# VectorE's scan ahead of a reciprocal, moments a step earlier, and one normalised tile ahead of ScalarE's sigmoids

## What is computed

```python
x = x + 0.5 * ffn(layernorm(x), w_up, w_down)
x = x + rnn(layernorm(x), Wf, Wi, Wh)
x = x + 0.5 * ffn(layernorm(x), w_up, w_down)
```

## Time and profile before

| what | value |
|---|---|
| median of 3 runs | 279.79 us (277.55 to 280.13) |
| the profiled execution's own time | 279.18 us |
| its span in the trace | 277.5 us |
| TensorE busy | 242.3 us (87%) |
| VectorE busy | 234.5 us (85%) |
| ScalarE busy | 222.4 us (80%) |
| GpSimd busy | 218.0 us (79%) |

### The profile page before, as it was taken

How to read it: one execution, slowest core, us unless ns; L and a number is a source line. 1 busy time by engine, 2 the same in 40 slices (tenths; PEclk the granted TensorE clock), 3 DMA queues, 4 the chain that set the end, 5 groups by cost and what they waited for, 6 DMA issues and landing times.

```text
span 277.5 us, 9737 instructions
## 1 busy us (share of the span) xinstructions
PE 242.3 (87%) x3757; PEld 168.2 (61%) x3757; DVE 234.5 (85%) x741; ACT 222.4 (80%) x546; POOL 218.0 (79%) x394
## 2 busy tenths in 40 slices
PE   0578999999999998899999956669999999999983
PEld 0335777777777776555554524236777778767863
DVE  3668699999998999799999946678899999998784
ACT  1256999999999999588888863568999999999971
POOL 4888688988978775788888888897889999997131
PEclk9999999999999999999999999889999999999999
DMA  6990000000000000000000000000021121112213
GB/s 180 269 259 5 4 4 2 2 2 4 2 6 0 2 5 1 4 1 0 2 1 0 0 1 0 2 2 2 16 64 40 41 65 56 40 40 61 59 40 116
DMA packets 18046, 9.73 MB, mean 35 GB/s; under 512 B 592, under 2 KB 17872, under 8 KB 18000
## 3 DMA queue, kind: packets, MB, share of 16 engines
q1 hardware_dynamic: 16896, 8.39, 10.9%
q10 hardware_dynamic: 1104, 0.72, 0.9%
HBM read 4.92 MB, written 4.19 MB: 33 GB/s over the span
## 4 chain that ended last, share of the span: by engine, by line
PE 62%; DVE 11%; POOL 11%; issue 7%; ACT 7%; DMA 1%; POOLq 0%; DVEq 0%; ACTq 0%
PE Y L443 16%; PE U L403 9%; PE G L430 9%; PE U L404 8%; PE U L458 7%; PE T L384 6%; POOL root L192 4%; PE Y L458 3%; ACT h_hi L299 3%; DVE X L580 2%; POOL inject L231 2%; ACT U L293 2%; DVE h_lo L564 2%; PE G L422 2%; PE G L467 2%
## 5 line engine op out<-in xcount | busy, mean ns | idle before, releaser
L564 DVE SCALAR_TENSOR_TENSOR h_lo<-h_hi,U 128x1024 f16<-128x1024 f16 x64 | 77.1, 1216 | 11.3 <-ACT h_hi L299 10.9
L293 ACT ACTIVATE U<-U 128x1024 f32<-128x1024 f32 x64 | 65.6, 1025 | 17.7 <-PE U L404 16.8
L213 POOL TENSOR_SCALAR xn<-X,neg_mean,rstd 128x128 f32<-128x128 f32 x164 | 72.8, 457 | 4.7 <-DVE rstd L555 2.2
L299 ACT ACTIVATE h_hi<-U 128x1024 f16<-128x1024 f32 x64 | 65.8, 1027 | 1.1
L443 PE MATMUL Y<-down_w,h_hi 128*128 128x128 f16 x512 | 60.9, 220 | 0.0
L443 PE MATMUL Y<-down_w_half,h_lo 128*128 128x128 f16 x512 | 60.6, 219 | 0.0
L403 PE MATMUL U<-xt_hi,up_w 128*128 128x512 f16 x128 | 50.7, 396 | 6.3 <-DVE h_lo L564 4.1
L192 POOL TENSOR_TENSOR root<-mv,half 128x8 f32<-128x8 f32 (+1 forms) x26 | 50.4, 1940 | 2.2
L220 POOL TENSOR_TENSOR rms<-ssq,half 128x4 f32<-128x4 f32 x32 | 32.2, 1008 | 24.0 <-ACT square_junk L325 24.0
L404 PE MATMUL U<-xt_lo,up_w 128*128 128x512 f16 x128 | 50.5, 395 | 0.0
L443 PEld LDWEIGHTS Y<-down_w_half,h_lo 128*128 128x128 f16 x512 | 50.1, 98 | 0.0
(11 more groups left out here) (71 smaller groups left out, 383.6 us busy)
## 6 DMA issues: line engine op xcount, KB each, us to landing
X<-in_L_attn_x SPq DMA_DIRECT2D x16, 256.0 KB, 5.4
out_x<-X SPq DMA_DIRECT2D x16, 256.0 KB, 2.5
up_raw<-in_L_ffn_w_up ACTq DMA_DIRECT2D x1, 256.0 KB, 4.1
down_raw<-in_L_ffn_w_down ACTq DMA_DIRECT2D x1, 256.0 KB, 5.0
gate_raw<-in_L_attn_Wh ACTq DMA_DIRECT2D x1, 64.0 KB, 4.4
gate_raw<-in_L_attn_Wi ACTq DMA_DIRECT2D x1, 64.0 KB, 4.1
gate_raw<-in_L_attn_Wf ACTq DMA_DIRECT2D x1, 64.0 KB, 4.2
```

Source lines behind the costliest of these rows:

```text
L213: m = eng.tensor_scalar(xn[:, n % 2, t, :], X[:, c, :], neg_mean[l][:, c:c + 1], rstd[l][:, c:c + 1], ALU.add, ALU.mult)
L293: eng.activation(U[part][:], U[part][:], ACT.Gelu, scale=1.0 / XN_SPLIT).then_inc(gelu_done, 1)
L299: eng.mul(h_hi[:, F % 2, 2 * part:2 * part + 2, :], U[part][:], H_SPLIT).then_inc(h_hi_done, 1)
L564: vec.scalar_tensor_tensor(out=h_lo[:, F % 2, 2 * part:2 * part + 2, :], in0=h_hi[:, F % 2, 2 * part:2 * part + 2, :], scalar=-1.0 / H_SPL ...
```

## The change

Three things are written in another order; no instruction is added or removed, and none changes its size.

1. On VectorE the reciprocal of the third norm (`scales`), which stood ahead of `scan` and `candidate` in steps 29 to 32, stands behind them. In later steps it stays where it was.
2. The second norm's chain moves one step ahead: `rnn_scales` on GpSimd runs from step 12 on and not 13, `rnn_moments` on ScalarE from step 11 on and not 12, and `later_stats` on VectorE has its slow start (one tile a step) in steps 7 to 10 and not 8 to 11, and takes four tiles a step from step 11 on. So `later_stats` also ends one step earlier.
3. On ScalarE `norm_tile(..., 2)` stands ahead of the first sigmoid of a step; `norm_tile(..., 3)` stays behind the second.

```diff
@@ GpSimd
-                if 0 <= s - 13 < groups:
-                    rnn_scales(s - 13)
+                if 0 <= s - 12 < groups:
+                    rnn_scales(s - 12)
@@ ScalarE
-                if k >= 12:
-                    rnn_moments(k - 12)
+                if k >= 11:
+                    rnn_moments(k - 11)
             act.preload_act_table(ACT.Sigmoid)
             for r in range(groups):
                 turned(groups + r + 1)
+                if by_both(groups + r + 2):
+                    norm_tile(groups + r + 2, 2)
                 gate(r, 0)
                 gate(r, 1)
                 if by_both(groups + r + 2):
-                    norm_tile(groups + r + 2, 2)
                     norm_tile(groups + r + 2, 3)
                 gate(r, 2)
                 if r == 0:
                     sum_squares(groups - 1)
-                if r + 4 < groups:
-                    rnn_moments(r + 4)
+                if r + 5 < groups:
+                    rnn_moments(r + 5)
@@ VectorE
-                room = 0 if s < groups - 8 else 1 if s < groups - 4 else 4
+                room = 0 if s < groups - 9 else 1 if s < groups - 5 else 4
@@ VectorE, the loop over steps
-                if 0 <= s - 29 < groups:
+                if s > 2 * groups and 0 <= s - 29 < groups:
                     scales(s - 29, *links(2)[s - 29])
                 if 0 <= r - 1 < groups:
                     scan(r - 1)
...
                 if 0 <= r < groups:
                     candidate(r)
+                if 29 <= s <= 2 * groups:
+                    scales(s - 29, *links(2)[s - 29])
```

## The result

The changed kernel takes 272.39 us (median of 4 runs, 271.12 to 272.5), the kernel before 279.96 us beside it (4 runs, 277.55 to 280.27). The ratio is 0.9738, with a 95% interval of 0.9676 to 0.9799: faster by 2.6%. The forecast was 272.5 us. The profiled execution took 272.4 us, and its span fell from 277.5 to 270.7 us, by 6.8; between the medians the gain is 7.6 us.

What follows compares the result with a forecast made beforehand. TensorE was taken to pace most of the kernel, with a ScalarE loop in the body and a VectorE-GpSimd mutual wait in the last steps. Gains 3.1 + 4.1 - 0.5 = 6.7 us from 279.18 gave 272.5 us, range 270.6 to 276.0.

Steps and rivals of the forecast that it cites:

- Part 1, the body: Body of the recurrence: a step falls from 3.84 to 3.56 us, with VectorE the bound; gain 3.1 us.
- That cover: Body: VectorE falling behind TensorE hides the early tile's delay of the first sigmoid; without it, 0.15 us a step.
- Part 2, the last steps: Last four recurrence steps: GpSimd the bound, `inject` of group 12 to `h_lo` 20.7 us instead of 24.8; gain 4.1 us.
- the step of 5.66: Last steps, groups 14 and 15: GpSimd's sum 1.36 + 2.47 + (1.75 + 0.08) us, counted twice.
- Part 3, the first pass: First feed-forward pass: `later_stats` one step earlier adds 1.2 us of VectorE work before step 12; cost 0.5 us.
- between 0 and 0.3, taken as 0: Last pass: one step loses 1.19 us of VectorE work where TensorE is the bound; gain taken as 0.
- Does the gain survive the last pass? ... I count no loss.: Start of the last pass: GpSimd's 1.02 us pause before its first `rms` takes the difference; no loss.
- The body did not stay at 3.84: First rival: the early tile waits, so the body keeps 3.84 us a step; 275.6 us, chance 0.14.
- GpSimd's roots were not late: Rival, last steps: late roots bring VectorE to `den` as late as before, only `rnn_scales` counts; 275.3 us, chance 0.04.
- the first pass did not pay in full: Rival: first pass loses all 1.2 us and the last steps give only 2.9; 274.4 us, chance 0.12.
- No lock: Rival, last steps: VectorE's scan and GpSimd's roots exclude each other, four times 1.27 = 5.1 us; 277.6 us, chance 0.02.
- A slower recurrence: Rival: ScalarE paces the recurrence, each step longer by a 0.43 us tile, 6.0 us in all; 281.6 us, chance 0.03.

Runs made afterwards that it cites:

- the dose of VectorE work: The changed kernel plus one small VectorE bn_stats into a scratch tile in each of eleven recurrence steps: 274.82 us, ratio 0.9812 to the kernel before.
- the ten products: The changed kernel plus ten unread TensorE products of 512 columns in the pause ahead of the last pass's first `h_lo`: 270.74 us, ratio 0.9688 to the kernel before.
- VectorE's tiles: Best version: changed kernel with tiles 2 and 3 of the last pass's groups 0 to 2 normalised by VectorE, not GpSimd: 269.13 us, again 270.02 us.

## Why the prediction was right

**Part 1, the body: right, 3.4 us for a forecast of 3.1.** The loop turn, sigmoids, tiles, turn was broken, and VectorE became the bound, as the dose of VectorE work shows. The step fell to 3.51 and not 3.56: the two pieces of VectorE's sum came out at 1.18 + 2.35 = 3.53 and not 1.19 + 2.37, and `inject` 2 still stood 0.2 us further behind its candidate than `inject` 12. One sign of this part did not come: turns were to be 3.56 apart, and are 3.46, TensorE's own 3.48. In ten steps VectorE doesn't hold TensorE up; it is the bound of `inject`, and that is where the last steps begin. ScalarE's tile ends 0.12 before the turn and not "well before" it. "That cover", the growing distance by which VectorE falls behind TensorE, hid the early tile: the candidate waits for no sigmoid in the rows above. The roots were what the tile needed: without them the step is 4.335.

**Part 2, the last steps: right, 4.5 us for 4.1.** GpSimd runs without a wait between the steps. Of 4.53 us, change 1 gives 3.28 and change 2 gives 1.27. The mis-sized term is the step of 5.66, which measured 5.53. The sum kept 0.08 between the end of the tiles and the `inject`, 1.75 + 0.08 = 1.83; with the candidate early, the `inject` starts before the tiles' recorded end, 1.70 after their start (165.35 to 167.05). No row shows the 0.08: it was added on top of the earlier trace rows. That 0.13 stands in two steps and the same 0.12 in the first (4.68 for 4.80). The last stretch, `inject` to `h_lo`, came to 4.54, within the 4.9 that was given as a limit.

**Part 3, the first pass: right**, 0.46 measured for 0.5 (0.44 in the changed kernel). VectorE's pause, 0.75 in the earlier trace rows, has shrunk to 0.30 in the changed kernel, so it took 0.45 of the 0.7 of the three tiles, and not all of it. The other end of change 2, "between 0 and 0.3, taken as 0" in the last pass, measured 0.25. One row of the timeline of VectorE:

```profile
90.14 1.22 DVE L565 SCALAR_TENSOR_TENSOR h_lo<-h_hi,U 128x1024 f16<-128x1024 f16 x1 [0.30 <-ACT h_hi L299]
```

**The step that failed: "Does the gain survive the last pass? ... I count no loss."** In the profiled run 0.9 us were lost there. The step looked at GpSimd's pause of 1.02 alone, and that pause did go: the first `rms` of the changed kernel, at 184.94, has no idle time before it (it stands 1.05 before the second, which waits for ScalarE and so for the slow products). What it didn't look at was TensorE's clock. The trace of before had the low level too, but earlier, at 179 to 182 us, where TensorE had slack: behind it TensorE is idle for 1.15 and for 1.14 us. Whether the change causes the loss is not settled. Change 1 makes TensorE's pause longer, 2.62 for 1.14. But the last pass also starts low in three kernels without change 1 (pauses of 0.68 to 1.14), and at the full level with changes 1 and 2 (2.63). Among the nine traces with neither the ten products nor VectorE's tiles, seven start low: the trace of before was one of the two that didn't. So part of the 0.9 is what that one trace happened to be spared. That the low level costs about a microsecond in the changed kernel, and that it can be kept away, is shown by the ten products. The price isn't fixed: with change 2 alone and with change 3 alone it lasts some 6.8 us in the trace and not 3.4, and costs 1.9 and 1.6.

**The rivals.** The body did not stay at 3.84, GpSimd's roots were not late, and the first pass did not pay in full. No lock was seen: with VectorE's scan of 162.83 beside the roots of 163.45 in the changed kernel, 1.27 and 1.64 us, both have their usual length. A slower recurrence is real, as change 3 alone shows, but not with change 2 beside it, and not quite by the rival's mechanism. The sigmoids, candidate and `inject` do follow the tile in one line, but ScalarE doesn't pace it: it stands 1.15 us for `shift`, the wait that the first rival named and priced at no loss. That its 0.49 a step is near the rival's 0.43, the length of a tile, is chance.

The sizes sum to 3.36 + 4.53 - 0.43 - 0.9 + 0.25 = 6.8 us, for 6.7 forecast: body and tail were each some 0.3 to 0.4 too small, and the clock took that back. The forecast also started from the profiled 279.18, 0.8 below the median of before; between medians the gain is 7.6. The agreement to 0.1 us is in part luck.

## What to carry to other kernels

When two engines wait for each other in turn, look for an instruction that waits on the one with urgent work queued behind it, and put that work first; then size the gain as the other engine's own sum of instructions. A move that gains nothing by itself can be the condition of another, so a bundle of changes has to be tried in its combinations: here 2 alone gave 0.0%, 3 alone +2%, both together -1.2%. A change can also gain in its own stretch and lose that to TensorE's clock in the next, so compare traces stretch by stretch. Where an engine has become the bound of a stretch, look at what its neighbours do while they wait: handing VectorE two of GpSimd's four tiles brought 2.4 us more, 1.7 of it in the steps themselves.

## What the runs showed of the hardware

**The same pause of TensorE, two outcomes.** Near the start of the kernel all thirteen traces have a pause of 2.07 to 2.48 us ahead of the `up` of the second group; the products before it, at 13 to 19 us, are 0.43 us apart in all of them. Timelines of TensorE, first the changed kernel, then the same kernel in a second execution:

```profile
21.88 0.38 PE L404 MATMUL U<-xt_hi,up_w 128*128 128x512 f16 x1 [2.33 <-DVE h_lo L565]
...
24.19 0.63 PE L405 MATMUL U<-xt_lo,up_w 128*128 128x512 f16 x1
24.62 0.63 PE L404 MATMUL U<-xt_hi,up_w 128*128 128x512 f16 x1
```

```profile
21.84 0.38 PE L404 MATMUL U<-xt_hi,up_w 128*128 128x512 f16 x1 [2.08 <-DVE h_lo L565]
...
23.57 0.38 PE L404 MATMUL U<-xt_hi,up_w 128*128 128x512 f16 x1
23.79 0.38 PE L405 MATMUL U<-xt_lo,up_w 128*128 128x512 f16 x1
```

In ten traces the products come 0.43 apart for a while, and VectorE's first add is at 35.42 to 35.87 us; in three they stay 0.22 apart, and it is at 34.17 to 34.30. So the draw at the start is worth some 1.3 us, about as much as the four runs of the changed kernel differ (271.12 to 272.5), and it lies ahead of everything that the change moves. The kernel before has these half-rate products too (22.53, 22.95, 23.38), though its granted clock reads 1.00 in that stretch: at such places the distance of equal products tells more than the clock column. The Trainium skill, "TensorE: Matmul & The Clock Gate", section "Part 1: The HAM clock gate (the "warmup" mystery)", says that the stretches over which the chip judges TensorE's activity run freely and don't begin with the kernel, so that the point of change differs from run to run. The traces agree that it differs, with 2.08 us of pause followed by either level; they don't show the reason.

**VectorE and GpSimd in SBUF side by side.** VectorE's two tiles in the best version read and write SBUF while GpSimd does its roots: 0.58 to 0.60 us for two. The root takes 1.65, as it does without them, and the tiles begin while it runs. No row has VectorE's tiles without a root beside them, so a stretch of the tiles themselves is not ruled out.
